# A 32-step delta-rule attention and gated MLP kernel: another order in the first part of a step

## The reference

```
xl = layernorm(x)
h  = layernorm(xl) * dn_g + dn_b
q, k, v = split(h @ gates_w + gates_b); lr = h @ lr_w + lr_b
k = k / norm(k)
u = solve_triangular(tril(k k^T, -1) + I, v)
xl = xl + ((q k^T) (lr * u)) @ out_w + out_b
xl = xl + relu((layernorm(xl) * mn_g + mn_b) @ w1 + b1) @ w2 + b2
x  = x + xl
out = x + (silu(n @ w_gate^T) * (n @ w_up^T)) @ w_down^T      with n = layernorm(x)
```

## Time and profile before

| | |
|---|---|
| three executions, median | 1578.6 us (1577.91 to 1579.26) |
| the profiled execution | 1577.6 us, span 1575.9 us |
| granted TensorE clock, mean | 0.998 |
| busy share: TensorE matmul, weight load | 98%, 86% |
| busy share: VectorE, ScalarE, GpSimd | 75%, 50%, 50% |
| HBM traffic | 112 GB/s over the span |

### The profile page before, as it was taken

One profiled execution on the slowest core, in us unless ns is written; L12 is line 12 of the kernel. 1 busy time (PEld: TensorE's weight loads), 2 busy tenths in 40 slices (PEclk: granted clock), 3 DMA queues, 4 the chain that ended last, 5 costly groups with the idle time before them and its releaser, 6 DMA issues.

```text
span 1575.9 us, 30053 instructions
## 1 busy us (share of the span) xinstructions
PE 1538.7 (98%) x10694; PEld 1354.9 (86%) x10694; DVE 1182.4 (75%) x3103; ACT 794.5 (50%) x1600; POOL 781.2 (50%) x918
## 2 busy tenths in 40 slices
PE   8999998899999999999999999999999999999998
PEld 7999997788888888888888888888888888888887
DVE  6767874578887777888877778888877777777774
ACT  6878774354444444444444444444444444444442
POOL 5456872244444554444445544444444444444442
PEclk9999999999999999999999999999999999999999
DMA  7999997112222322222222222222222222222200
GB/s 241 340 311 314 327 330 247 61 61 74 75 74 75 114 74 75 74 75 74 74 75 98 91 74 74 70 67 72 73 94 82 75 74 74 75 74 74 69 20 27
DMA packets 150166, 178.20 MB, mean 113 GB/s; under 512 B 78850, under 2 KB 132098, under 8 KB 141826
## 3 DMA queue, kind: packets, MB, share of 16 engines
q1 hardware_dynamic: 150018, 176.28, 34.0%
HBM read 98.64 MB, written 77.59 MB: 112 GB/s over the span
## 4 chain that ended last, share of the span: by engine, by line
PE 60%; DVE 15%; ACT 4%; POOL 3%; issue 2%; ACTq 0%; DVEq 0%; POOLq 0%
PE ps L175 31%; PE ps L1102 15%; PE ps L1112 5%; PE ps L1033 4%; DVE xinv L1408 3%; DVE bs L1602 3%; DVE xh2T_lo L1463 2%; PE ps L1008 2%; ACT work L1319 2%; POOL sc L1620 2%; DVE a L1597 2%; DVE late L1488 1%; DVE gl_hi L1513 1%; ACT hh L1284 1%; PE ps L1022 1%
## 5 line engine op out<-in xcount | busy, mean ns | idle before, releaser
L1674 POOL TENSOR_TENSOR hl<-late,hh 128x512 fp32r<-128x512 f32 x128 | 165.6, 1294 | 206.0 <-ACT hh L1284 206.0
L1279 ACT ACTIVATE late<-ps 128x512 f32<-128x512 f32 x192 | 114.5, 596 | 170.4 <-PE ps L1102 170.4
L1112 PE MATMUL ps<-wdT,hh 128*128 128x256 f32 x744 | 197.7, 303 | 0.0
L1458 DVE TENSOR_TENSOR late<-ps,late 128x512 f32<-128x512 f32 x192 | 132.7, 691 | 84.9 <-PE ps L1102 83.1
L1288 ACT ACTIVATE z_hi<-ps 128x256 fp32r<-128x256 f32 x128 | 49.2, 384 | 290.7 <-PE ps L1033 290.2
L1112 PE MATMUL ps<-wdT,hl 128*128 128x256 f32 x744 | 181.2, 281 | 0.3 <-DVE hl L1463 0.3
L1284 ACT ACTIVATE hh<-late 128x512 fp32r<-128x512 f32 x192 | 120.8, 629 | 108.9 <-DVE late L1458 108.9
L1620 POOL TENSOR_TENSOR sc<-ls,mhalf 128x4 f32<-128x4 f32 x64 | 65.1, 1018 | 194.5 <-DVE ls L1425 194.5
L1102 PE MATMUL ps<-xh3T_hi,wgT 128*128 128x512 f32 x384 | 153.6, 400 | 1.1 <-DVE xh3T_lo L1463 1.1
L1102 PE MATMUL ps<-xh3T_lo,wuT 128*128 128x512 f32 x384 | 152.2, 396 | 0.0
L1102 PE MATMUL ps<-xh3T_lo,wgT 128*128 128x512 f32 x384 | 152.0, 396 | 0.0
(11 more groups left out here) (216 smaller groups left out, 4703.0 us busy)
## 6 DMA issues: line engine op xcount, KB each, us to landing
xhT_scratch<-xhTk SPq DMA_DIRECT2D x32, 1024.0 KB, 6.2
xhT<-xhT_scratch SPq DMA_DIRECT2D x32, 1024.0 KB, 6.4
gg_scratch<-late SPq DMA_DIRECT2D x32, 640.0 KB, 4.1
gg<-gg_scratch SPq DMA_DIRECT2D x32, 640.0 KB, 3.9
xk<-in_L_attn_x_dram SPq DMA_DIRECT2D x32, 512.0 KB, 5.4
xt<-in_L_attn_x_dram SPq DMA_DIRECT2D x32, 512.0 KB, 4.1
out_dram<-late SPq DMA_DIRECT2D x31, 512.0 KB, 2.9
low_scratch<-late SPq DMA_DIRECT2D x128, 16.0 KB, 2.7
```

What stands on the lines that cost most here:

```text
L1112: mm = pe.matmul(ps[:, (FG, FU)[j // 2], (j % 2) * C:(j % 2 + 1) * C], part[:, h, blk(j)], wdT[:, h, :], start=(h == 0 and part is hh), st ...
L1279: act.activation(sg[:, h % 2, :], ps[:, FG, :], ACT.Silu, scale=QUANT).then_inc(sg_ev[h], 1)
L1458: dve.tensor_tensor(hf[:, h % 2, :], ps[:, up_bank(h), :], sg[:, h % 2, :], ALU.mult).then_inc(hf_ev[h], 1)
L1674: pool.tensor_tensor(hl[:, h, :], hf[:, h % 2, :], hh[:, h, :].bitcast(F32), ALU.subtract).then_inc(hl_ev[h], 1)
```

## The change

- Normed rows: group 1 of xn goes from GpSimd to VectorE, at the head of VectorE's step (semaphore xh2_first). Of the second norm groups 2 and 3 go from VectorE to ScalarE (xh3_rest), for which VectorE makes the shift -mean x rstd (ln3_shift, 128 x 4 elements).
- TensorE: the transposes of the first norm stand before row block 1; block 5 of the down product of row group 3 stands behind w block 0 and bt block 2. In steps without a down product (i = 0 and 1) row blocks 1 and 2 stand before the transposes and row block 3 before the MLP; in step 1 there are 21, 7 and 6 filler products (`keep_busy`) between them.
- VectorE: gl's rounded copy goes behind row block 2, the first output sum behind w block 2, the lane steps of a step to other places, one half of x2's second sum behind w block 1, z block 0's remainder before the second output sum.
- ScalarE takes over xhm's rounded copy, before z block 2.
- GpSimd: the sum xa + a0 (L1651) stands before gl's remainder (L1642).

```diff
 pe_body
-                    if att:
-                        pe.wait_ge(pT_ev, i + 1)
-                        after(pe, m2_sum, i)
-                        pe_row_block(pe, A1, 1, xa_ps)
+                    if att and not down:
+                        if i == 1:
+                            keep_busy(pe, S0, 21)
+                        pe_row_block(pe, i, 1)
                         pe_weights(pe, i, 1)
+                        if i == 1:
+                            keep_busy(pe, S0, 7)
+                        pe_row_block(pe, i, 2)
+                        pe_weights(pe, i, 2)
+                        if i == 1:
+                            keep_busy(pe, S0, 6)
                     if mlp:
+                        pe.wait_ge(xh2_first, i)
                         pe.wait_ge(xh2_done, i)
                         pe.wait_ge(xh2_rest, i)
...
                         pe_transposes(pe, (FO0, FO1), xn, t2_ps)
+                    if att and down:
+                        pe_row_block(pe, i, 1)
                     if down:
                         pe_down(pe, i, 0, (HB - 1,))
                         pe_down(pe, i, 1)
-                    if att:
-                        pe.wait_ge(xa_ev, i + 1)
-                        pe_row_block(pe, A0, 2, xb_ps)
-                        pe_weights(pe, i, 2)
+                    if att and down:
+                        pe_row_block(pe, i, 2)
+                    if att and not down:
+                        pe_row_block(pe, i, 3)
+                        pe_weights(pe, i, 3)
                     if mlp:
                         after(pe, hf_ev[HB - 2], i - 1)
                         pe_mlp1(pe, i, 0)
-                    if att:
-                        pe.wait_ge(xb_ev, i + 1)
-                        pe_row_block(pe, A1, 3, x128_ps)
-                        pe_weights(pe, i, 3)
+                    if att and down:
+                        pe_row_block(pe, i, 3)
...
                     if down:
-                        pe_down(pe, i, 3)
+                        pe_down(pe, i, 3, range(HB - 1))
                     if att:
                         pe_wstep(pe, i, 0)
                         pe_bt(pe, i, 2)
+                    if down:
+                        pe_down(pe, i, 3, (HB - 1,))
+                    if att:
                         pe_zstep(pe, i, 0)
 act_body
                     if att:
+                        act.wait_ge(xhm_done, TB * (i + 1))
+                        after(act, bt_ps, i)
+                        act.activation(xhm2[0][:, :, :], xh[:, :, :], ACT.Copy).then_inc(xhm_hi, 1)
                         act_z(act, i, 2)
                         act_weights(act, i, (5,))
                         act_z(act, i, 1)
                         act_weights(act, i, (6,))
+                    if mlp:
+                        act.wait_ge(ln3_shift, i)
...
+                        for j in range(2, TB):
+                            act.wait_ge(x2_ev[j], i)
+                            op = act.activation(xn[:, j, :], x2s[i % 2][:, j, :], ACT.Identity,
+                                                scale=sc3[:, 0, j:j + 1], bias=sc3[:, 1, j:j + 1])
+                        op.then_inc(xh3_rest, 1)
+                    if att:
                         act_z(act, i, 0)
 dve_body
+                    if mlp:
+                        dve.wait_ge(l2[2], i)
...
+                        dve.tensor_scalar(xn[:, 1, :], a0[:, 1, :], mv2[:, 1, 0:1], sc2[:, 0, 1:2],
+                                          ALU.subtract, ALU.mult).then_inc(xh2_first, 1)
                     if att:
                         masked(dve, i)
                     if down:
                         dve_hl(dve, i - 1, HB - 1)
                     if att:
+                        row_block(dve, i, 1)
+                        if not down:
+                            row_block(dve, i, 2)
+                    if mlp:
+                        dve_lo(dve, xh2T2[1], xh2T2[0], (FO0, FO1), t2_hi, t2_ev, i)
+                    if att:
+                        if down:
+                            row_block(dve, i, 2)
                         wait(dve, gg_in, i * 16)
                         after(dve, w_ps[0], i)
                         dve.tensor_copy(gl2[0][:, :], gg[:, 0:OFF]).then_inc(gl_hi, 1)
-                        row_block(dve, A1, 1, xa_ps, xa_ev, i)
+                        row_block(dve, i, 3)
...
+                    dve_invert(dve, m, r, 0, 1)
+                    if att:
+                        dve_z(dve, i, 3)
+                    if mlp:
+                        dve_h1_lo(dve, i, 1)
+                    if att:
+                        dve_w(dve, i, 2)
                     if down:
                         dve_out(dve, i, 0)
...
                     if att:
                         dve_z(dve, i, 1)
-                    dve_invert(dve, m, r, 3, 4)
+                    dve_invert(dve, m, r, 1, 2)
                     if mlp:
                         dve.wait_ge(ln3_done, i)
+                        after(dve, xh3_rest, i - 1)
+                        dve.scalar_tensor_tensor(out=sc3[:, 1, :], in0=mv3[:, :, 0], scalar=-1.0, in1=sc3[:, 0, :],
+                                                 op0=ALU.mult, op1=ALU.mult).then_inc(ln3_shift, 1)
...
-                        dve_xh3(dve, i, range(2))
+                        dve_xh3(dve, i, range(1))
                     if att:
                         dve_w(dve, i, 0)
                     if mlp:
-                        dve_xh3(dve, i, range(2, TB)).then_inc(xh3_done, 1)
+                        dve_xh3(dve, i, range(1, 2)).then_inc(xh3_done, 1)
+                    dve_invert(dve, m, r, 2, 3)
+                    if att:
+                        dve_z(dve, i, 0)
                     if down:
                         dve_out(dve, i, 1)
-                    if att:
-                        dve_z(dve, i, 0)
+                    dve_invert(dve, m, r, 3, 4)
                     if mlp:
                         dve_lo(dve, x3l, x3h, (FO0, FO1), x3h_ev, x3l_ev, i)
 pool_body
-                        for j in range(2):
-                            op = pool.tensor_scalar(xn[:, j, :], a0[:, j, :], sc2[:, 0, j:j + 1], sc2[:, 1, j:j + 1],
-                                                    ALU.mult, ALU.add)
-                        op.then_inc(xh2_done, 1)
+                        pool.tensor_scalar(xn[:, 0, :], a0[:, 0, :], sc2[:, 0, 0:1], sc2[:, 1, 0:1],
+                                           ALU.mult, ALU.add).then_inc(xh2_done, 1)
                     if r == 0:
                         wait(pool, inv_out, 32 * m)
                         invert_start(pool, lanes, m)
-                    if att:
-                        pool.wait_ge(gl_hi, i + 1)
-                        pool.tensor_tensor(gl2[1][:, :], gg[:, 0:OFF], gl2[0][:, :].bitcast(F32),
-                                           ALU.subtract).then_inc(gl_lo, 1)
                     if mlp:
...
                         pool.wait_ge(xb_done, i)
                         pool.tensor_tensor(xa2[:, :, :], xa[:, :, :], a0[:, :, :], ALU.add).then_inc(xa_done, 1)
+                    if att:
+                        pool.wait_ge(gl_hi, i + 1)
+                        pool.tensor_tensor(gl2[1][:, :], gg[:, 0:OFF], gl2[0][:, :].bitcast(F32),
+                                           ALU.subtract).then_inc(gl_lo, 1)
```

More of the change, by code:

```diff
@@ L1001, in up_bank, with row_bank @@
                 return (FU, S0)[h % 2]
+            def row_bank(f):
+                return (A1, A0, A1)[f - 1]
             with nc.Block() as block:
@@ L1015, in pe_level, with pe_row_block @@
                     mm.then_inc(done, 1)
-                def pe_row_block(pe, bank, f, done):
+                def pe_row_block(pe, i, f):
+                    pe.wait_ge((pT_ev, xa_ev, xb_ev)[f - 1], i + 1)
+                    if f == 1:
+                        after(pe, m2_sum, i)
                     rows = slice(f * SUB, (f + 1) * SUB)
                     for j in range(TB):
-                        mm = pe.matmul(ps[j * SUB:(j + 1) * SUB, bank, 0:f * SUB], p1[:, j, rows], xinv[:, j, 0:f * SUB],
-                                       start=True, stop=True)
-                        mm.then_inc(done, 1)
+                        mm = pe.matmul(ps[j * SUB:(j + 1) * SUB, row_bank(f), 0:f * SUB], p1[:, j, rows],
+                                       xinv[:, j, 0:f * SUB], start=True, stop=True)
+                        mm.then_inc((xa_ps, xb_ps, x128_ps)[f - 1], 1)
                 def pe_zstep(pe, i, j):
@@ L1228, in pe_body @@
                         pe.wait_ge(xh3_done, i)
+                        pe.wait_ge(xh3_rest, i)
                         for j in range(TB):
@@ L1354, in act_body @@
                         act_weights(act, i, (6,))
+                    if mlp:
+                        act.wait_ge(ln3_shift, i)
+                        for k in range(CB):
+                            act.wait_ge(t2_ps[k], i)
```

(20 more changed lines are left out.)

22 lines of the change are left out of this document (7 added, 15 removed).

## The result

| | before | after |
|---|---|---|
| median of four executions | 1578.4 us (1577.9 to 1579.3) | 1633.0 us (1631.6 to 1634.0) |
| profiled execution: time, span | 1577.6, 1575.9 us | 1634.0, 1632.2 us |
| granted TensorE clock, mean | 0.998 | 0.996 |

The ratio is 1.0345, with a 95% interval of 1.0327 to 1.0363. The prediction said 1620.1 with a range of 1574 to 1631: slower, as it came out, but by 42 us where it was 55, and 2 us over the top of the range.

What follows compares the result with a forecast made beforehand. TensorE, busy 98% of the span, was taken as the bound. 11 x 1.27 + 17 x 1.6 - 0.6 + 1.9 - 1.0 = +41.5 us on 1578.6 gave 1620.1, range 1574 to 1631.

Steps and rivals of the forecast that it cites:

- Items 1 and 2: Front of step: single normed rows win 0.25 us; GpSimd's early sum (L1651) holds VectorE's hl, stalling TensorE 1.7 us.
- Items 1, 3 and 5: Step without lane work: down block 5 0.25 earlier, row block 3 1.06 late, second half loses 0.21; 1.27 us longer.
- rival C: Full steps: hl runs beside L1651 without stall, a step wins 0.34 us without lane work; 1570 us; chance 0.17.
- Item 4: xhm's rounded copy on ScalarE before z block 2: takes 1.1 us, hidden in idle time, cost 0.
- Item 6: Steps with lane work: fourth lane step waits for GpSimd's next sum, remainders 0.6 us later; 1.6 us longer a step.
- The steps i = 8 and 16: GpSimd's memset at their start puts the sum behind hl: -0.3 us each.
- rival B: Front of step: VectorE's own normed row also loses against GpSimd; 1.0 us more in 28 steps, 1648 us; chance 0.05.
- Item 7: Second step with 34 filler products: +1.9 us, bounds -1.6 and +5, clock stays up; first step and tail -1.0.
- The ends: First step and tail: two chains that get shorter, -1.0 us.

Runs made afterwards that it cites:

- experiment 1: The changed kernel with one wait more: GpSimd's sum of xa and a0 starts only when VectorE's hl of block 5 is done; 1587.6 us.
- experiment 2: The changed kernel with GpSimd's sum of xa and a0 cut into two halves in its place, no wait added; 1598.5 us.
- experiment 3: The kernel before with only GpSimd's order changed: the sum of xa and a0 ahead of gl's remainder; 1645.8 us.
- experiment 7: Single parts: on Experiment 6, xhm's copy on VectorE 1573.3 us, block 5 back 1570.6; on Experiment 5, two GpSimd rows 1585.0; kernel before, rows shared only, 1584.5.
- Experiment 5: On top of experiment 1, the fourth lane step moved behind the remainders of the second transposes, the sixth one place later; 1575.0 us.
- Experiment 6: On top of Experiment 5, GpSimd's memset of the lanes moved behind its sum of xa and a0; 1571.7 us.

## Why the prediction was right or wrong, point by point

- *Items 1 and 2 (the single rows, the stall).* The mechanism held: the sum starts behind the single row, hl ends 0.55 behind the sum, TensorE waits 1.42 in 30 steps (1.24 in one of them), experiment 1 gives it back by the time at which hl may run, and experiment 2 gives back 1.08 (41.10 to 40.02). The Trainium skill, "SBUF — State Buffer", section "Who interferes with whom", says that the first to come has the shared ports for its whole instruction and the other stands still. The halves of experiment 2 and both sides of the race in experiment 3 agree (2.91 for 2.39 on GpSimd, 2.75 for 0.55 and 2.94 for 0.69 on VectorE).
- *Items 1, 3 and 5: the net right, the gain at the front mis-sized.* Net 1.27 was forecast for a step without lane work and 1.33 measured. hl ends when it was said to end (4.75 us into the step for 4.78), row block 2 comes 1.43 late for 1.36 and row block 3 1.15 for 1.06, and the rest loses 0.18 for 0.21. But block 5 of the down product, forecast 0.25 earlier than before, comes 0.02 earlier (3.26 us into the step for 3.28). The transposes start at 2.04 for 1.95, since VectorE's row takes 0.58 beside GpSimd's and not 0.41. And from there to block 5 it is 1.22, where I had counted 1.08: with row block 1 between them the transposes, the row block and the down product follow one another at 0.20 and 0.13. The stall hides this 0.23, since it ends with hl and not earlier. It shows where the stall is gone: in experiment 1 a step wins 0.09 (39.77 to 39.68), where rival C had 0.34, and so the stall itself costs 1.42, where my terms made it 1.61. Block 5 of the fourth down product costs 0.12 by its move (experiment 7), for the 0.02 of 0.20 won and 0.22 lost.
- *Item 4.* Held: ScalarE's copy takes 1.07, hidden, and moving it is worth nothing (experiment 7).
- *Item 6, mis-sized.* The mechanism was right. The steps with lane work lost 1.84, not 1.6: beside the 0.06 of every step the held lane step costs 0.75 (41.85 against 41.10), where the terms gave 0.57. Experiment 5 gives it back. In the sum 4 us.
- *The steps i = 8 and 16, the step that failed.* "-0.3 each", since the memset would hold the sum back behind hl. It holds VectorE's row as well (1.47 for 0.58), so the transposes start 0.89 later than in the other steps (2.93 us into the step for 2.04), and hl, behind that row in the same queue, meets the sum after all. Experiment 6 removes the 0.9; in the kernel of experiment 3, where VectorE has no row, these two steps do escape (40.56 and 40.57 where the others take about 42). 4.6 us. In rival B I had asked whether the row waits for L1651, not whether it waits for the memset; and its first half, that the row loses against GpSimd's row, is true in the full steps (0.58 for 0.41). The page "VectorE: DVE Perf Modes" of the Trainium skill, section "Mode 2×_2P — use both read ports for one tensor", puts such instructions with one tensor among those that may take both ports; the traces agree in that both this row and gg's copy (2.75 for 0.55) are held. My reason against it was the row's rate; whatever the rate means, it did not tell whether the row is held.
- *Item 7, the step that failed most.* The second step was 0.6 over. The ends were forecast at -1.0, by their shorter chains, and gave +3.9, by TensorE's granted clock: that fell to half twice (2.4 to 1.2 GHz), for 10.2 us in the first step and for 3.4 behind the stall of the last full step. These are windows of the changed kernel:

```profile
267.50:275.50 8.00, 7.07 (x28) 6.12 (x28) 1.99 (x6) 3.50 (x6) 4.94 (x3) 0.50 0.32 88
...
1552.50:1556.50 4.00, 3.44 (x22) 3.05 (x23) 2.54 (x7) 2.13 (x5) 0.00 (x0) 0.60 0.00 0
```

  TensorE had been stopping and starting ahead of both (2.56 busy of 3.50 before the first, the stall of 1.4 before the second). The first is not fixed to the change: ten more kernels here have TensorE's new order in the first step and ran it in 29.5 (five) or 30.6 to 30.8 (five), never in 32.6. The three profiles with the old first step show 29.8 each; whether the new order makes this fall likelier stays open. Nor does the miss hang on it: the execution with the highest mean clock, 0.999, which leaves room for some 3 us at half (an estimate: twice 0.001 of 1630), took 1631.6 us. Where the clock stayed the term had the right sign: in experiment 6 first step, last full step and drain together are 0.7 shorter than before, 0.1 of it by the full step. The second fall went with the stall (experiment 1: last full step and drain 81.1 for 84.2).
- *Range.* Its upper end of 1631 was taken from the stall and from item 7. The steps with lane work (4.0 us over), the steps i = 8 and 16 (4.6) and the ends (4.9, by the clock) had no bounds of their own, and it stopped short of rival B, though a part of what B says came true.

## What to carry to other kernels

A transfer of work between VectorE and GpSimd, or an earlier start of either, is priced by who shares the memory at that moment: list for each GpSimd instruction the next VectorE instructions that read or copy within SBUF, and the one behind those. An early start on an idle engine may be a loss, and a wait that holds it back a gain (45 us here). Two edits paid only together. The shared rows alone cost 0.10 a step, the rest of the change without them 0.28 (40.05 for 39.77, with the sum behind hl), and both together win 0.09 (39.68).

The best version found is the changed kernel with the sum behind hl, the lane step and the memset moved and block 5 of the down product in its old place: 1570.6 us, 0.9939 of the kernel before (0.9924 to 0.9954).

## What the runs showed of the hardware that I had not expected

- A held instruction shows no idle time: its wait lies inside its duration (hl 2.38, row 1.47, copy 2.75). Only a duration above the least of its form gives it away, and the least can be rare: in the changed kernel the row takes 0.58 in 28 of its 32 executions and 0.41 in two.
- VectorE instructions with one SBUF input and an SBUF output are held too, and by a memset (row 1.47 for 0.58, above) as well as by a sum; hl, with two inputs, is not held by the memset: at 929.97 in experiment 3 both start together, and hl takes 0.69, as it does beside both memsets of the kernel before.

```profile
929.97 0.69 DVE L1463 TENSOR_TENSOR hl<-late,hh 128x512 fp32r<-128x512 f32 x1 [0.36 <-ACT hh L1284]
930.58 0.76 DVE L1513 CAST gl_hi<-gg 128x768 fp32r<-128x768 f32 x1
```

```profile
929.97 0.95 POOL L184 MEMSET inv<- 128x1024 f32 x1
```

- A race decided within 0.03 us by the records fell out differently from step to step: in experiment 3 the copy of gg is held in 8 of the full steps, hl in 20.
